# B and C of a selective scan from one projection of 128 raw rows and paired 64-row products, the two scan halves in turn

## The reference, cut to what matters

```python
xz = x @ W_in                            # x: the normed rows, 128 wide; W_in 128 x 512
xi, z = jnp.split(xz, 2, axis=-1)        # 256 each
proj = xi @ W_xp                         # 256 x 129
delta = jax.nn.softplus(proj[..., :1])
B_raw = proj[..., 1:1 + D_STATE]         # 64 columns
C_raw = proj[..., 1 + D_STATE:]          # 64 columns
B = B_raw @ W_B                          # 64 x 256
C = C_raw @ W_C
A_bar = jnp.exp(delta * -jnp.exp(A_log))
h = _scan_recurrence(broadcast(A_bar), B * xi)   # h_t = a_t h_{t-1} + b_t along the 512 rows
y = C * h + D * xi
y = y * jax.nn.silu(z)
return y @ W_out
```

## Time and profile before

| | |
|---|---|
| median of 3 runs (lowest to highest) | 1116.2 us (1115.88 to 1116.23) |
| the profiled execution | 1117.61 us |
| its span, first to last instruction | 1116.1 us |
| TensorE busy | 1061.7 us (95%) |
| VectorE busy | 933.6 us (84%) |
| ScalarE busy | 696.0 us (62%) |
| GpSimd busy | 249.0 us (22%) |
| mean granted clock of TensorE | 0.992 |

### The profile page before, as it was taken

The page is one execution under the profiler, slowest core; times in us unless marked ns, Lnnn a source line. Parts: engine busy times, 40 slices in busy tenths (PEclk is TensorE's granted clock), DMA queues, the critical chain, the costliest instruction groups (busy, mean ns, idle before and its releaser), DMA issues. The chain is left out here.

```text
span 1116.1 us, 18645 instructions
## 1 busy us (share of the span) xinstructions
PE 1061.7 (95%) x5980; PEld 668.1 (60%) x5980; DVE 933.6 (84%) x2077; ACT 696.0 (62%) x1509; POOL 249.0 (22%) x235
## 2 busy tenths in 40 slices
PE   6999999999999999999999999999999999999995
PEld 3665657566565665657566565665657566565663
DVE  6797896979889797897979889797997979889677
ACT  4593846738386592846738385582846749285582
POOL 0040310313122031310303121031311303131086
PEclk9999999999999999999999999999999999999998
DMA  3000000000000000000000000000000000000435
GB/s 145 19 2 10 1 19 10 0 28 0 19 9 19 9 0 28 0 19 9 0 28 0 19 9 19 9 0 28 0 19 9 0 28 0 19 9 19 170 94 161
DMA packets 31907, 27.61 MB, mean 25 GB/s; under 512 B 1552, under 2 KB 25744, under 8 KB 31760
## 3 DMA queue, kind: packets, MB, share of 16 engines
q1 hardware_dynamic: 31888, 27.37, 7.5%
HBM read 15.57 MB, written 11.80 MB: 25 GB/s over the span
## 5 line engine op out<-in xcount | busy, mean ns | idle before, releaser
L1752 POOL TENSOR_TENSOR pair<-pair,cgt 128x512 f32<-128x512 f32 x64 | 94.7, 1508 | 525.3 <-DVE pair L1515 525.3
L984 ACT ACTIVATE gx<-p 128x512 f32<-128x512 f32 x256 | 147.2, 596 | 27.7 <-PE p L538 21.3
L536 PE MATMUL p<-x1Th,Gl 128*128 128x512 f32 x256 | 120.4, 470 | 0.3 <-ACT gx L984 0.3
L939 ACT ACTIVATE gelu<-p,bias_u 128x512 f32<-128x512 f32 x32 | 22.0, 687 | 157.8 <-PE p L483 157.8
L538 PE MATMUL p<-x1Th,Gh 128*128 128x512 f32 x256 | 101.2, 395 | 0.0
L537 PE MATMUL p<-x1Tl,Gh 128*128 128x512 f32 x256 | 101.0, 395 | 0.0
L647 PEld LDWEIGHTS p<-vbd,pair 128*128 128x128 f32 x512 | 62.0, 191 | 41.2 <-issue 26.8
L1782 POOL TENSOR_TENSOR skip<-skip,W 128x512 f32<-128x512 f32 x15 | 19.2, 1277 | 295.0 <-DVE skip L1296 295.0
L610 PE MATMUL p<-gx,x1T 128*32 128x512 f32 x512 | 68.2, 604 | 12.0 <-DVE pair L1526 11.2
L622 PE MATMUL p<-nodesT,K 128*128 128x512 f32 x128 | 66.7, 603 | 12.7 <-DVE nodesT L1488 12.7
L647 PE MATMUL p<-vbd,pair 128*128 128x128 f32 x512 | 74.0, 288 | 0.0
(11 more groups left out here) (267 smaller groups left out, 2701.6 us busy)
## 6 DMA issues: line engine op xcount, KB each, us to landing
xin<-in_x SPq DMA_DIRECT2D x16, 256.0 KB, 2.8
hx_scratch<-vdw SPq DMA_DIRECT2D x15, 256.0 KB, 2.6
res_scratch<-res SPq DMA_DIRECT2D x14, 256.0 KB, 2.0
gx<-in_weights SPq DMA_DIRECT2D x1, 1216.0 KB, 10.1
vp<-hx_scratch SPq DMA_DIRECT2D x4, 256.0 KB, 3.4
GT<-res_scratch SPq DMA_DIRECT2D x4, 256.0 KB, 3.3
out<-vp SPq DMA_DIRECT2D x4, 256.0 KB, 3.2
W<-in_weights SPq DMA_DIRECT2D x1, 746.0 KB, 11.1
```

Source lines behind the costliest of these rows:

```text
L536: pe.matmul(head_bank(h)[:, :], tile(Gl, h), x1Th[:, :], start=True, stop=False)
L984: act.activation(tile(gx, h, T), head_bank(h)[:, :], ACT.Copy).then_inc(R["gx_copied"], 1)
L1752: pool.tensor_tensor(pw, pw, spread(cgt[:, H * n:H * n + H].unsqueeze(2), [128, H, CHUNK]), ALU.subtract)\
```

## The change

B and C are no longer folded with W_xp W_B and W_xp W_C. The setup folds only W_in W_xp into `Mraw`, 128x128: 64 columns give the raw rows of B, 64 those of C. In each pass one product (`scan_raw`) gives all 128 raw rows, ScalarE copies them to SBUF (`raw_copy`, into `sp0`, which `delta` has done with), and for each half q two products of 64 rows follow (`scan_bc`): B from rows 0 to 63, C from rows 64 to 127, into two banks. W_B and W_C (`WBC`) therefore stay in SBUF for the whole run. On VectorE the halves are done one after the other: product with B and scan of half 0, then of half 1, then both products with C.

```diff
-        MBC = sb("MBC", 2 * INNER)
-        MB, MC = MBC[:, 0:INNER], MBC[:, INNER:2 * INNER]
+        Mraw = sb("Mraw", 128)
...
-            def inner_products():
...
+            def inner_weights():
+                for q in range(2):
+                    mm = pe.transpose(P1[3][:, 128 * q:128 * q + 128], w("WxpT", 128 * q, 128 * q + 128), ident)
                 mm.then_inc(R["setup_ps"], 1)
...
-                        mm = pe.matmul(P1[2 - n][:, 0:256], w("WinT", 128 * q, 128 * q + 128),
-                                       tile(y, n, 512)[:, 256 * q:256 * q + 256], start=(q == 0), stop=(q == 1))
...
+                    mm = pe.matmul(P1[2][:, 0:128], w("WinT", 128 * q, 128 * q + 128), y[:, 128 * q:128 * q + 128],
+                                   start=(q == 0), stop=(q == 1))
...
-            def scan_b(j):
-                project(j, 0, "delta_ready", j + 1, MB[:, 0:128], "b0_ps")
-                project(j, 1, "xi0_ready", j + 1, MB[:, 128:256], "b1_ps")
-
-            def scan_c(j, q):
+            def scan_raw(j):
+                project(j, 0, "delta_ready", j + 1, Mraw[:, :], "raw_ps")
+
+            def scan_bc(j, q):
+
+                low, high = slice(0, 64), slice(64, 128)
                 if q == 0:
-                    project(j, 2, "xi1_ready", j + 1, MC[:, 0:128], "c0_ps")
+                    pe.wait_ge(R["raw_ready"], j + 1)
+                    pe.wait_ge(R["xi1_ready"], j + 1)
                 else:
-                    project(j, 0, "bx0_ready", j + 1, MC[:, 128:256], "c1_ps")
+                    pe.wait_ge(R["xi0_ready"], j + 1)
+                    pe.wait_ge(R["bx0_ready"], j + 1)
+                pe.matmul(P0[(0, 1)[q]][:, :], w("WBC", 128 * q, 128 * q + 128)[low, :], raw[low, :], start=True, stop=True)\
+                    .then_inc(R[f"b{q}_ps"], 1)
+                pe.matmul(P0[(2, 0)[q]][:, :], w("WBC", 128 * q, 128 * q + 128)[high, :], raw[high, :], start=True, stop=True)\
+                    .then_inc(R[f"c{q}_ps"], 1)
...
+            def raw_copy(j):
+                act.wait_ge(R["raw_ps"], j + 1)
+                act.activation(raw[:, :], P0[0][:, :], ACT.Copy).then_inc(R["raw_ready"], 1)
...
                 if later(j):
-                    act.wait_ge(R["delta_ready"], j)
+                    act.wait_ge(R["c1_ps"], j)
...
                     decay(j)
+                    raw_copy(j)
...
                 if j is not None:
-                    scan_inputs(j)
+                    scan_half(j, 0)
                 if i is not None:
                     pair_weights(i, 0)
                 if j is not None:
-                    scans(j)
+                    scan(j, 0)
+                    scan_half(j, 1)
+                    scan(j, 1)
+                    scan_out(j, 0)
+                    scan_out(j, 1)
```

More of the change, by code:

```diff
@@ L202, in build @@
         end_res = free[9:18] + [tile(GT, n, T) for n in range(4)] + [lam[:, 0:T], res[:, :], x1[:, :]]
-        c_out = sp0
+        c_out = raw = sp0
         P0 = [psum(f"p0_{n}") for n in range(3)]
@@ L372, in fold_heads @@
                     else:
-                        pe.wait_ge(R["setup_ev"], 6 if order == 1 else 4)
+                        pe.wait_ge(R["setup_ev"], 3 if order == 1 else 4)
                 else:
@@ L850, in first @@
                 act.wait_ge(R["setup_ps"], 3)
-                for n in range(2):
-                    cp = act.activation(tile(y, n, 512), P1[3 + n][:, :], ACT.Copy)
-                cp.then_inc(R["setup_ev"], 1)
+                act.activation(y[:, 0:256], P1[3][:, 0:256], ACT.Copy).then_inc(R["setup_ev"], 1)
                 xi_copy(0)
@@ L856, in first @@
                 decay(0)
+                act.wait_ge(R["setup_ps"], 4)
+                act.activation(Mraw[:, :], P1[2][:, 0:128], ACT.Copy).then_inc(R["setup_ev"], 1)
                 fold_heads(0, 0)
-                scan_weights()
+                raw_copy(0)
                 gelus()
@@ L1269, in first @@
                 expert_sums()
-                scan_inputs(0)
-                scans(0)
+                scan_half(0, 0)
+                scan(0, 0)
+                scan_half(0, 1)
+                scan(0, 1)
+                scan_out(0, 0)
+                scan_out(0, 1)
                 gate0(0, 0)
@@ L1361, in delta, with scan_half, scan, scan_out @@
                     .then_inc(R["delta_ready"], 1)
[L1363 to L1372, removed]
-                dve.wait_ge(R["decay0_ready"], j + 1)
[L1374 to L1378, removed]
-                    dve.wait_ge(R[f"c{q}_ps"], j + 1)
-                    dve.wait_ge(R[f"h{q}_ready"], j + 1)
-                    dve.tensor_tensor(tile(y, q, T), P0[bank][:, :], tile(y, q, T), ALU.mult)\
-                        .then_inc(R[f"ch{q}_ready"], 1)
+            def scan_half(j, q):
+                if q == 0:
+                    if later(j):
+                        dve.wait_ge(R["out0_ps"], j)
+                dve.wait_ge(R[f"b{q}_ps"], j + 1)
+                dve.wait_ge(R[f"xi{q}_ready"], j + 1)
+                dve.tensor_tensor(tile(y, q, T), P0[q][:, :], tile(xi, q, T), ALU.mult).then_inc(R[f"bx{q}_ready"], 1)
+            def scan(j, q):
+                dve.wait_ge(R["decay0_ready"], j + 1)
+                dve.wait_ge(R[f"bx{q}_ready"], j + 1)
+                dve.tensor_tensor_scan(tile(y, q, T), decay0[:, :], tile(y, q, T), 0.0, ALU.mult, ALU.add)\
+                    .then_inc(R[f"h{q}_ready"], 1)
+            def scan_out(j, q):
+                dve.wait_ge(R[f"c{q}_ps"], j + 1)
+                dve.wait_ge(R[f"h{q}_ready"], j + 1)
+                dve.tensor_tensor(tile(y, q, T), P0[(2, 0)[q]][:, :], tile(y, q, T), ALU.mult)\
+                    .then_inc(R[f"ch{q}_ready"], 1)
             def gate0(j, q):
```

46 lines of the change are left out of this document (17 added, 29 removed).

## The result

The changed kernel takes 1132.3 us (median of four runs, 1127.08 to 1136.58) against 1116.2 us before (1115.88 to 1117.15): a ratio of 1.0143, 95% interval 1.0122 to 1.0164. It is slower, as forecast (1127.7, range 1119.5 to 1134), by 16 us where 11.5 were forecast. Two of the four runs lie above the top of the range. They form two groups, 1127.1 and 1128.7, 1135.8 and 1136.6, with mean granted clocks of 0.993, 0.988, 0.983 and 0.984. The profiled execution is the slowest of them, with a span of 1135.1.

What follows compares the result with a forecast made beforehand. It took each pass as bound first by VectorE, then by TensorE. Loop +11.9, start-up -1.7 and clock +1.3 gave +11.5 on 1116.2, so 1127.7 us, range 1119.5 to 1134.

Steps and rivals of the forecast that it cites:

- What bounds the kernel: In each loop pass VectorE is the bound up to L1526, then TensorE up to the next running sums.
- VectorE's order, +0.79 a pass: In the loop, the second B product leaves free cover (+0.61) and the second scan depends on it (+0.18).
- The pair at 0.86: On TensorE in the loop, two 64-row products overlap and last 0.86 us, saving 0.86 a pass.
- TensorE's wait before L580: In the loop this wait for ScalarE's copy grows from 0.33 to about 1.2 us, so nothing is gained.
- No gain from less TensorE work: In the loop, TensorE's 0.86 us saved a pass goes into waits off the path: zero gain.
- no cost from the raw copy: ScalarE's copy in each pass, 0.59 us, fits into 1.21 idle: zero cost.
- The clock in the loop, +1.3: TensorE's idle spells halve the clock in one or two passes, up to 0.86 us each; bounds 0 and +6.9.
- The start-up, -1.7: In the setup, replacing `scan_weights` and three full projections saves 1.7 us; bounds 0 and -3.4.
- The sum of 11.5: Whole kernel: loop +11.9, start-up -1.7 and clock +1.3 make +11.5 us; bounds +5.6 and +19.7.
- upper clock term in the loop: Upper bound for clock falls in the loop: eight of the 15 passes, +6.9 us.
- The rivals: TensorE the bound (1101.6, 6%); delay absorbed (1114.5, 6%); no pair overlap (1127 to 1130, 7%); clock mostly falls (1139.3, 6%).
- The third: Rival: a pair's products in the loop do not overlap, the delay is covered, total 1127 to 1130 us; 7%.

Runs made afterwards that it cites:

- E4: The changed kernel with C's products on rows 0 to 63 too, so the two products of a pair run one after the other: 1137.2 us.
- E11: E7 with `pair_levels(3)` moved ahead of `pair_scores(3)` on TensorE: 1107.1 us, ratio 0.9917 to the kernel before.
- E2: The kernel before with only VectorE's new order in the loop; TensorE, ScalarE and start-up as before: 1127.1 us, ratio 1.0097.
- E12: E8 with `pair_levels(3)` moved ahead of `pair_scores(3)` on TensorE: 1108.1 us.
- E8: E1 with six unused products added in TensorE's start-up pauses: 1114.0 us, ratio 0.9984 to the kernel before.
- E7: The kernel before with four unused products added in TensorE's start-up pauses: 1114.7 us, ratio 0.9984 to the kernel before.
- E3: The changed kernel with two unused products filling one start-up pause of TensorE, ahead of the fold that waits for the bias: 1128.9 us.
- E5: The changed kernel with six unused products added in TensorE's start-up pauses: 1126.1 us.
- E6: E5 with two more unused products in each pass, ahead of TensorE's waits for the left halves and before L622: 1124.6 us.
- E1: The changed kernel with VectorE's old order in the loop, which also takes the second pair apart: 1119.5 us, ratio 1.0043 to the kernel before.
- E10: E8 with `gate_u(1)` moved ahead of `pair_scores(3)` on TensorE: 1113.8 us.

## Why the prediction was right or wrong, point by point

**What bounds the kernel: right.** The two parts of a pass, VectorE's and TensorE's, were read from two waits. E4 (1.7 us more TensorE work in VectorE's part, pass unchanged) and E11 (0.86 us moved out of TensorE's part, pass 0.6 shorter) show it from both sides. One wait of VectorE for TensorE is missing in the prediction, the longest: 3.0 us in each pass for the sum that ends the first layer,

```profile
DVE x L1400 <- PE p L496: 27.0, 9, 3.0
```

It lies in TensorE's part and speaks for the division.

**VectorE's order, +0.79 a pass: right in place and size.** The wait at `pair_weights(0)` went from 0.18 to 0.78. The second scan starts 0.76 behind the product that it reads, where an unrelated operation had started 0.61 behind; from L1524 to the first operation of `top1` it is 5.62 us, 0.79 more than before. With the order alone the scan starts 0.70 behind that product (E2). The pass is 0.81 longer, and 0.75 with the order alone.

**The pair at 0.86: too small, without effect.** It takes 1.06, and 1.91 if the two can't overlap. The 0.20 are not lost by running side by side: the lone 64-row product of E12 takes 1.05 at the same place. Three projections became 0.86 + 1.06 ahead of L610, a saving of 0.66 and not 0.86. Hence TensorE's wait before L580 is 0.54 on the matmul side and 0.9 on the side of the weight loads, not 1.2. The Trainium skill, "TensorE: Matmul & The Clock Gate", section "Measured speedup vs the span model", gives a pack the duration of one product and some 4 ns for each further one. With 1.05 for the one, from E12, that is an estimate of 1.06 for the pair, and the trace, with 1.06, agrees. Its section "The mechanism" keeps matmuls in the order of the program. Taken for the passes of a float32 product, as the prediction took it, that isn't borne out: the upper product's first pass starts at 482.26, the lower one's second at 482.79.

**No gain from less TensorE work, no cost from the raw copy: right.** The changed kernel against E2 shows the first, 0.46 us less TensorE work a pass and no shorter pass, and E4 shows it from the other side. E8 against E7 shows the second, 0.7 us apart in total with equal passes.

**The clock in the loop, +1.3: the right size where it came.** The profile of the changed kernel has one fall in 15 passes (+1.1), that of E3 three (+2.3), those of E5, with the same idle spells, and of E4 and E6, with less idle time there, none. Which pass it hits differs from run to run.

**The start-up, -1.7: the step that failed.** It went to +6.2 in the profiled execution. The working took over one spell of half clock, the one of the earlier trace rows, and priced only the raw projection at it. It took 0 as the worst case, the case in which nothing is gained. In fact the spell doesn't end where it ended before. The changed kernel's profile has a pause of 2.08 us ahead of it and two further waits of TensorE in it, each for a product of VectorE that must free the bank:

```profile
18.75 1.75 PE L374 MATMUL p<-gx 64*128 64x128 f32 x8 [2.08 <-DVE bias_u L1197]
...
27.14 1.19 PE L462 MATMUL p<-sp,W 64*128 64x512 f32 x1 [0.93 <-DVE y L1373]
...
29.97 2.07 PE L444 MATMUL p<-xnT,W 128*128 128x512 f32 x2 [0.75 <-DVE y L1373]
```

The clock stayed at 1.2 GHz for 23.9 us, up to 43. That the half clock comes with idle time is shown: with the pauses filled (E5, E8) the scatter is gone. The pause ahead of L374 is the one that it follows in the profiles, and its length differs between executions of the same setup. The clock fell behind 2.08 (changed) and 1.65 (E4, and the kernel before), not behind 1.31 (E1) nor, with before's setup, 1.09 (E2):

```profile
18.84 1.13 PE L374 MATMUL p<-gx 64*128 64x128 f32 x8 [1.31 <-DVE bias_u L1201]
```

Why the clock then stays down is open. The two further waits don't explain it: they stand in E3 too (1.00 and 0.75), whose clock didn't fall, and E4, with the pause of 1.65 that the kernel before has as well, stayed down for 30.7 us without them. Without the long half clock the term would have been near its forecast: the profiled start-up of E1 is 56.3, that of E2 with before's setup 57.5, a difference of -1.2. The sum of 11.5 would so have been met by runs like the one of 1127.1. The median lies between the two groups. That the range held it is owed to its upper clock term in the loop, which is not what happened, and so is luck. The bounds of the terms give 1121.8 to 1135.9; the range stated was wider below and, for no reason given, narrower above.

**The rivals.** None of the four came. The third, no overlap at all, is what E4 brings about, and there the pass stays the same, as that rival said. The range's own scatter, 10 us from run to run, was no part of any of them.

## What to carry to other kernels

A busy share of 95% says little where two engines take turns in being the bound. Find in each part which wait ends last, and price a change by the part that it lies in. Work that an engine does where it would otherwise wait for a result is free, and moving it behind that wait costs its whole length. An experiment that undoes one part of a change should be checked for what else it undoes: E1, E8, E10 and E12 took a pair apart. In a start-up, where idle time and half clock meet, give a term a lower and an upper bound that include the clock staying low.

## What the runs showed of the hardware

- Two float32 products of 64 rows x 512 columns on the two halves of the rows run beside each other at almost no cost: 1.06 us for the pair, 1.05 for one alone at the same place (E12), 1.91 for two on the same rows (E4). But one of 64 rows between products of 128 takes longer than one of 128 rows there, 1.05 against 0.86.
- Once TensorE's granted clock had fallen to 1.2 GHz in the start-up, it stayed there for 23.9 us in one profile and 30.7 in another (E4), for 21 us of it with TensorE busy without a gap (E4, 20 to 41 us). In the kernel before it was back after 3.4 us. With the pauses filled it didn't fall. What distinguishes the busy stretches in which it rose from those in which it didn't wasn't tried and is open.
- Unused products in pauses of TensorE cost nothing and made a kernel's runs agree: 1125.5 to 1126.3 instead of 1127.1 to 1136.6.
